# A softmax pass in a graph network: GpSimd weights half of the features, and a dense pipeline starts its newest group first

## The reference

```python
x_j = h[dst] + ee                       # h = x @ W_lin + b_lin, ee = edge_attr @ W_edge + b_edge, two heads of 64
alpha = (x_i * att_i).sum(-1) + (x_j * att_j).sum(-1)
alpha = jnp.where(alpha >= 0, alpha, NEG_SLOPE * alpha)
e = jnp.exp(alpha - segment_max(alpha, src, N)[src])
alpha = e / (segment_sum(e, src, N)[src] + 1e-16)
out = segment_sum(x_j * alpha[:, :, None], src, N).mean(axis=1) + bias
x = _layernorm(x + out)
```

## Time and profile before

| what | before |
|---|---|
| median of 3 runs | 10380.73 us |
| lowest and highest | 10374.76 and 10389.13 us |
| profiled execution, first to last instruction (its span) | 11537.7 us |
| DVE busy | 6821.8 us, 59% |
| POOL busy | 6567.8 us, 57% |
| ACT busy | 4714.2 us, 41% |
| PE busy | 3146.5 us, 27% |

### The profile page before, as it was taken

One profiled execution on the slowest core, in us unless ns is written; L12 is line 12 of the kernel. 1 busy time (PEld: TensorE's weight loads), 2 busy tenths in 40 slices (PEclk: granted clock), 3 DMA queues, 4 the chain that ended last, 5 costly groups with the idle time before them and its releaser, 6 DMA issues. The chain is left out here.

```text
span 11537.7 us, 92744 instructions
## 1 busy us (share of the span) xinstructions
PE 3146.5 (27%) x19432; PEld 2586.9 (22%) x19432; DVE 6821.8 (59%) x9436; ACT 4714.2 (41%) x6523; POOL 6567.8 (57%) x6626
## 2 busy tenths in 40 slices
PE   1111588882000000000023555555554200000002
PEld 1111477772000000000013444444443100000001
DVE  6777666664222311159962777777775566666664
ACT  1111466661211111137731666666662343334342
POOL 5656666665677777730023666666662466666663
PEclk9999767675555555555555677776775655555555
DMA  3332322222333323235522444444441666666662
GB/s 91 88 83 78 80 60 71 71 82 26 121 112 111 107 94 106 103 125 207 205 104 52 117 118 124 117 116 122 118 117 39 194 202 201 199 202 205 203 201 70
DMA packets 722783, 1395.92 MB, mean 121 GB/s; under 512 B 409552, under 2 KB 439453, under 8 KB 715095
## 3 DMA queue, kind: packets, MB, share of 16 engines
q0 software_dynamic: 287072, 587.19, 19.4%
q1 hardware_dynamic: 406786, 639.32, 17.0%
q10 hardware_dynamic: 28852, 168.65, 4.0%
HBM read 827.48 MB, written 602.51 MB: 124 GB/s over the span
## 5 line engine op out<-in xcount | busy, mean ns | idle before, releaser
L822 POOL DMA_INDIRECT l_rows<-in_x,l_idx x1568 | 1613.7, 1029 | 1010.1 <-issue 431.0
L2445 POOL DMA_INDIRECT l_rows<-table,l_idx x1568 | 1487.5, 949 | 1032.2 <-issue 483.2
L1925 POOL DMA_INDIRECT l_rows<-h,l_idx x1568 | 1540.3, 982 | 882.1 <-issue 442.4
L1303 POOL DMA_INDIRECT rows<-l_rows,l_idx x1568 | 1548.9, 988 | 554.0 <-issue 526.3
L1960 PE MATMUL l_made<-l_kv_w,l_rows_t 128*128 128x256 f32 x3136 | 1117.3, 514 | 1041.1 <-ACT l_kv L1990 402.5
L1960 PEld LDWEIGHTS l_made<-l_kv_w,l_rows_t 128*128 128x128 f32 x3136 | 761.2, 259 | 1279.5 <-issue 1147.1
L2521 ACT ACTIVATE l_lifted<-l_rows,l_up 128x256 f32<-128x256 f32 x1568 | 653.2, 463 | 824.0 <-DVE l_half_low L2473 527.1
L1698 PE MATMUL l_wide<-l_diag,l_ones 128*128 128x384 f32 x4 | 3.3, 926 | 3218.0 <-DVEq L1728 3218.0
L1259 ACT COPY l_rows<-l_run 128x1792 f32<-128x1792 f32 x56 | 191.6, 3421 | 1636.1 <-POOLq L88 1359.5
L1292 DVE TENSOR_TENSOR l_rows<-l_run,l_weights_ps 128x56 f32<-128x56 f32 x56 | 12.0, 215 | 1371.0 <-POOLq L88 1168.7
L1698 PEld LDWEIGHTS l_wide<-l_diag,l_ones 128*128 128x128 f32 x4 | 1.0, 312 | 3218.9 <-DVEq L1728 3218.9
(11 more groups left out here) (393 smaller groups left out, 12672.9 us busy)
## 6 DMA issues: line engine op xcount, KB each, us to landing
sums<-l1s_out ACTq DMA_DIRECT2D x56, 1988.0 KB, 7.1
sums<-l_out SPq DMA_DIRECT2D x112, 924.0 KB
spread<-zeros SPq DMA_DIRECT2D x28, 3612.0 KB
l_spread<-spread SPq DMA_DIRECT2D x112, 903.0 KB
l1s_rows<-rows SPq DMA_DIRECT2D x56, 1008.0 KB, 4.7
spread<-zeros SPq DMA_DIRECT2D x56, 938.0 KB
l_spread<-spread SPq DMA_DIRECT2D x56, 938.0 KB
sums<-l_out ACTq DMA_DIRECT2D x56, 896.0 KB
```

The lines of the kernel that those rows point to most:

```text
L822: pool.indirect_dma_start(rows[:, b, t], None, a["x"], bass.IndirectOffsetOnAxis(ap=idx[:, b, t:t + 1], axis=0)) \
L1303: pool.indirect_dma_start(g["rows1_d"], bass.IndirectOffsetOnAxis(ap=idx[:, b, t:t + 1], axis=0), rows[:, b, t], None).then_inc(sent[b], 16)
L1925: pool.indirect_dma_start(rows[:, c.r, t, 0:C], None, g["h2_d"], bass.IndirectOffsetOnAxis(ap=idx[:, c.r, t:t + 1], axis=0)).then_inc(got[ ...
L2445: pool.indirect_dma_start(rows[:, b, t], None, g["table3_d"], bass.IndirectOffsetOnAxis(ap=idx[:, b, t:t + 1], axis=0)) \
```

## The change

**In the softmax pass** each part's two products are made by two engines and its scan is cut in two.

- DVE weights the features for head 0 only (`weighed_low`, PSUM), and raises the new semaphore `begun` behind the copy of the last column. GpSimd weights those for head 1 (`weigh`), into `weighed_high`, which is the second head's half of the old `scale` tensor in SBUF. It may write part n when `begun` says that DVE has left the scans of the part before last, and when the exponentials are there.
- `scale_low` stays in SBUF; the scales of head 1 go to `scale_high`, a single buffer in PSUM.
- DVE scans head 0 (2030 elements), waits for GpSimd (`high_weighed`) and for ACT (`high_ready`), and scans head 1 (2030 elements).
- ACT makes the scales in two functions. `low` is as before for one head. `high` waits for the end of the last part's second scan, since the buffer is single, copies that part's last column (a new instruction, 70 elements), and then writes `scale_high`. The order of ACT's turn becomes high(c,1), exponentials, store(c,0), low, high(c+1,0), store(c,1), low(c+1,1).
- `rows_used` now counts two engines. DVE clears `scale_high` once at the start.

```diff
-                        for head in range(H):
-                            last = v.tensor_tensor(data[:, head, :, 1:].rearrange("p f t -> p t f"), rows[:, b, at, 0:F],
-                                                   exp[:, b, 1, head, at].unsqueeze(2).to_broadcast([P, T, F]), ALU.mult)
-                        last.then_inc(rows_used[b][n], 1)
-                        v.tensor_copy(data[:, :, :, 0:1], run[:, 1 - n, :, :, T:T + 1])
-                        wait(v, scale_ready[n], c.at + 1)
+                        v.tensor_tensor(weighed_low[:, :, 1:].rearrange("p f t -> p t f"), rows[:, b, at, 0:F],
+                                        exp[:, b, 1, 0, at].unsqueeze(2).to_broadcast([P, T, F]), ALU.mult).then_inc(rows_used[b][n], 1)
+                        v.tensor_copy(weighed_low[:, :, 0], run[:, 1 - n, 0, :, T]).then_inc(begun, 1)
+                        wait(v, low_ready[n], c.at + 1)
                         wait(v, copied[n], c.at + 1)
                         v.drain()
...
+                        wait(v, high_weighed, c.at * PARTS + (n + 1))
+                        wait(v, high_ready[n], c.at + 1)
+                        v.tensor_tensor_scan(run[:, n, 1].rearrange("p f t -> p (f t)"), scale_high.rearrange("p f t -> p (f t)"),
+                                             weighed_high[:, n].rearrange("p f t -> p (f t)"), 0.0, ALU.mult, ALU.add).then_inc(scanned[n], 1)
                         v.drain()
...
+                def weigh(c, n):
+                    at = slice(n * T, (n + 1) * T)
+                    wait(pool, exp_ready[c.b], c.h + 2)
+                    if not (isinstance(c.g, int) and c.at == 0 and n == 0):
+                        wait(pool, begun, c.at * PARTS + n)
+                    pool.tensor_tensor(weighed_high[:, n, :, 1:].rearrange("p f t -> p t f"), rows[:, c.b, at, 0:F],
+                                       exp[:, c.b, 1, 1, at].unsqueeze(2).to_broadcast([P, T, F]), ALU.mult).then_inc(rows_used[c.b][n], 1)
+                    pool.drain().then_inc(high_weighed, 1)
...
+                def high(c, n):
+                    wait(act, scanned[1 - n], c.at + (n + 1))
+                    nc.scalar.copy(weighed_high[:, n, :, 0], run[:, 1 - n, 1, :, T])
+                    nc.scalar.copy(scale_high[:, :, 1:], exp[:, c.b, 0, 1, n * T:(n + 1) * T].unsqueeze(1).to_broadcast([P, F, T])).then_inc(high_ready[n], 1)
...
                 def turn(c, after):
+                    high(c, 1)
+                    if after:
+                        exponentials(after)
                     store(c, 0)
                     if after:
-                        exponentials(after)
-                        scales(after, 0)
+                        low(after, 0)
+                        high(after, 0)
                     store(c, 1)
                     if after:
-                        scales(after, 1)
+                        low(after, 1)
```

**In the dense pipelines** the loop over the stages runs the other way, on PE and on ACT, so that at step s the newest group is turned first and the product of the group before follows:

```diff
         for step in range(len(self.groups) + self.stages - 1):
-            for k in reversed(range(self.stages)):
+            for k in range(self.stages):
```

**Between ordering and layer 0** stands a second `clear_semaphores`:

```diff
+        ordering(nc, a, sem, dict(locals()))
+        clear_semaphores()
         norm = Normalise(sem, "l01")
-        ordering(nc, a, sem, dict(locals()))
```

More of the change, by code:

```diff
@@ L1425, in source_order_sums @@
         exp = s.sb("l1s_exp", [P, 2, 2, H, S])
-        data = s.ps("l1s_data", [P, H, F, T + 1])
+        weighed_low, scale_high = (s.ps(f"l1s_{n}", [P, 4 * 512])[:, 0:F * (T + 1)].rearrange("p (f t) -> p f t", t=T + 1)
+                                   for n in ("weighed_low", "scale_high"))
+        scale_low, weighed_high = scale[:, :, 0], scale[:, :, 1]
         outb = s.sb("l1s_out", [P, PARTS, T, W + H])
@@ L1500, in _ @@
                 v.tensor_copy(tail[:, W:W + H], top[:, UNROLL - 1, :, S])
+            @block.gpsimd
+            def _(pool):
+                def weigh(c, n):
[6 more added lines that the diff above has]
+                    pool.drain().then_inc(high_weighed, 1)
+                pool.wait_ge(set_up, 1)
+                for r in range(UNROLL):
+                    for n in range(PARTS):
+                        weigh(Chunk(0, r), n)
+                with pool.Fori(1, NB // UNROLL) as q:
+                    for r in range(UNROLL):
+                        for n in range(PARTS):
+                            weigh(Chunk(q, r), n)
             @block.scalar
@@ L1511, in exponentials, with low @@
                     wait(act, exp_ready[c.b], c.h + 2)
-                def scales(c, n):
+                def low(c, n):
                     wait(act, scanned[n], c.at + 1)
-                    for head in range(H):
-                        last = nc.scalar.copy(scale[:, n, head, :, 1:], exp[:, c.b, 0, head, n * T:(n + 1) * T].unsqueeze(1).to_broadcast([P, F, T]))
-                    last.then_inc(scale_ready[n], 1)
+                    nc.scalar.copy(scale_low[:, n, :, 1:], exp[:, c.b, 0, 0, n * T:(n + 1) * T].unsqueeze(1).to_broadcast([P, F, T])).then_inc(low_ready[n], 1)
+                def high(c, n):
+                    wait(act, scanned[1 - n], c.at + (n + 1))
+                    nc.scalar.copy(weighed_high[:, n, :, 0], run[:, 1 - n, 1, :, T])
+                    nc.scalar.copy(scale_high[:, :, 1:], exp[:, c.b, 0, 1, n * T:(n + 1) * T].unsqueeze(1).to_broadcast([P, F, T])).then_inc(high_ready[n], 1)
                 def store(c, n):
@@ L1811, in scalar @@
         for step in range(len(self.groups) + last - 1):
-            for k in reversed(range(last)):
+            for k in range(last):
                 i = step - k
```

18 lines of the change are left out of this document (10 added, 8 removed).

## The result

The changed kernel takes 10198.83 us (median of 4 runs, 10194.06 to 10207.38) against 10383.55 for the kernel before in the same session: ratio 0.9821 [0.9807, 0.9835]. The forecast was 10232, its range 10180 to 10295. The time lies in the range and 33 us under the point, at the rival "TensorE's clock rises" (10194).

A forecast was written before the change was run, and what follows sets the result against it. VectorE was taken to bound the softmax pass, and waits between stages the output products. Terms -115 + 4 - 21 - 10 - 2.5 - 6 + 2 = -149 took 10380.7 to 10232 us, range 10180 to 10295.

The forecast's parts named there:

- TensorE's clock rises: Rival, faster: in both output products, gapless TensorE work raises the clock, -38 us over some 34 steps, 10194 us; chance 0.12.
- The pass: Softmax pass: VectorE's part falls from 13.4 to 11.35 us, a chunk to 26.0, -115 us over 56 parts.
- too slow: Rival, softmax pass: GpSimd's product exceeds 8.9 us and VectorE stands for the rest; at 13 us 10461; chance 0.05.
- half of it: Rival, softmax pass: GpSimd's product about 9.9 us or ScalarE at 27 us a chunk, +56, 10288 us; chance 0.11.
- taking turns: Rival, softmax pass: GpSimd and VectorE do not work together, only the pipelines gain, 10350 us; chance 0.03.
- The start of the pass: Softmax pass start: clearing 2030 elements 1.7 us, GpSimd's and VectorE's first products together +2; together +4 (1.7 to 9).
- the prediction's own sign of error: Softmax pass: the forecast is wrong if VectorE's product or scores lengthen beside GpSimd's product; no size given.
- The dense pipelines: Output products: the wait goes, step 2.63 instead of 3.50 us at clock 0.50; -21 in layer 1, -10 in layer 2.
- The MLP: MLP: nearly full already, with 0.21 us of wait a step; -2.5 us (0 to -3.9).
- The query product: Query product: GpSimd, issuing 49 transfers at 987 ns and more each, sets the pace; 0 us.
- The root product: Root product: waits 0.94 us a step but also stands 18.2 us at once; -6 us, between 0 and -11.
- The second clear: A second clear leaves VectorE idle for at most 2.23 us more; +2 us (0 to 2.2).

The follow-up runs named there:

- e1: Changed kernel with the old order of TensorE's and ScalarE's work in the pipelines, leaving the pass and the second clear: 10279.94 us against 10393.57, ratio 0.9895.
- e5: Changed kernel, VectorE signalling GpSimd at the start of its own product instead of after the copy behind it: 11603.07 us on a slower chip, ratio to before 0.9833.
- e6: Changed kernel with the first head's weighted features in SBUF instead of PSUM: 11659.38 us, ratio to the kernel before 0.9881.
- e2: Kernel before with only the new order in the pipelines: 10317.49 us against 10393.57, ratio 0.9931.
- e4: Kernel before, old order, two unread 128x128 products after each step's turns in layer 1's output product: that stage took 79.0 us.
- e10: Kernel before, old order, four unread 128x128 products after each step's turns in layer 1's output product: that stage took 57 us.
- e7: Changed kernel, TensorE's turns in layer 2's attention pass held until ScalarE's first scale copy of the chunk two before: 11577.15 us on a slow chip, ratio 0.9804.
- e11: Changed kernel, held-back attention turns, unread TensorE products up to the start of both output products: 11438.85 us against 11654.21 on a slower chip, ratio 0.9801.
- e0: The kernel before, unchanged, timed and profiled a second time: 10382.33 us.
- e8: The changed kernel, unedited, timed again over five rounds beside the kernel before: 10200.02 us against 10386.37, ratio 0.9826.
- e3: Changed kernel, ScalarE's store copy going through the running sums in the order of the output instead of the input: 10205.60 us, ratio 0.9826.
- e9: Changed kernel with held-back turns in the attention pass and 26 and 40 unread TensorE products ahead of the output products: 10156.01 us, ratio to before 0.9784.

## Why the prediction was right, and where it failed

**The pass: right, a little too small.** Forecast -115 us and +4 at its start, measured -119.5 from first to last scan (e1, with all but the pipelines: -114 in all). The part is 11.24 us and not 11.35: two waits behind the first scan cost nothing, since the second scan starts 0.08 us before the first one's end. GpSimd's product took 3.81 us where 4.4 was assumed between 2.2 and 8.6, and lay under the scan as the order said. So "too slow", "half of it" and "taking turns" did not happen. ScalarE waits 73.1 us for the scan, 12.3 of them once at the start; the other 60.8 / 26 = 2.3 us a chunk are what the sum had left (26.0 - 23.7).

**The start of the pass** had the collision, in another place than forecast: not the first products, but `scores` of the next chunk, where in the changed kernel a copy took 3.76 us instead of 0.23 and in e1 the instruction ahead of it 3.77:

```profile
4661.26 3.81 POOL L1516 TENSOR_TENSOR l1s_scale<-l1s_rows,l1s_exp 128x1960 f32<-128x1960 f32 x1 [24.66 <-ACT l1s_exp L1537]
4661.38 3.76 DVE L1466 COPY l1s_hold_data<-l1s_side 128x112 f32<-128x112 f32 x1
```

```profile
4674.84 3.74 POOL L1516 TENSOR_TENSOR l1s_scale<-l1s_rows,l1s_exp 128x1960 f32<-128x1960 f32 x1 [25.52 <-ACT l1s_exp L1537]
4674.88 3.77 DVE L1465 TENSOR_SCALAR l1s_hold_keep<-l1s_side 128x112 f32<-128x112 f32 x1 [1.93 <-DMA l1s_side<-spreada]
```

The Trainium skill's "SBUF — State Buffer", section "Who interferes with whom", has the two engines shut each other out for a whole instruction, copies among them, and lets the order of issue decide which one waits. These rows, e5 and e6 agree: GpSimd's product was held where VectorE's product or scan had started 0.01 to 0.05 us before it, and VectorE's small instruction where GpSimd's product had started 0.04 to 0.12 us before it. This second kind happened once in a run, for 3.5 us; it is also the prediction's own sign of error, that scores lengthen beside GpSimd's product, in a form too rare to matter.

**The dense pipelines: the step that failed.** The prediction priced the closed gap at the low clock alone. It kept TensorE at 0.50 and gave its rise a chance of 0.12, because TensorE had worked 20.99 of 21 us at 0.50 in another stage. In the new order the clock rises in both output products: -46.4 and -24.0 instead of -21 and -10. Of the 46.4 about 25 are the waits and the overlap of the kinds of product (25 steps of 3.44 at 2.45 us), the other 21 the clock; the runs on the order alone (e2, -76) and on the gap alone (e4, e10) bear it out. The row that spoke against it still stands: the stretch behind the root product has no gap and stays at 0.50 for 21 us in the changed kernel too, and the root product ahead of it, which keeps a wait of 0.16 us a step, stays at 0.50 for all of its 38 us. So a stretch without a gap may rise 4.5, 17 or 66 us in (7 to 22 us in layer 1's output product over the eight profiles with the new order), or not within 21, and one that didn't is weak evidence against. The rule of the Trainium skill's "TensorE: Matmul & The Clock Gate", Part 1, that sustained activity releases the throttle, deserved more than it got: both output products agree with it (granted clock 0.77 and 0.82), this one stretch does not.

**Smaller terms.** The step at the low clock was 2.45 us, not 2.63: the eight products take 1.60 us start to start when their weights are ready, not 1.77. The MLP gave 5.9 (forecast 2.5). The query product fell from 38 to 20 us where 0 was forecast, but the 48 transfers that GpSimd issues from its rows take 61.6 us in either kernel, as the prediction had it, and 7.0 is left of the whole stretch. The root product gave 8.7 (forecast 6), and the end of the kernel gave 8.3 of it back: GpSimd's last transfers end 66.1 us behind the start of the root product in both kernels (10243.1 to 10309.2 and 10056.9 to 10123.0), so the forecast's -6 should have been 0. Stalls like the 18.18 us of the earlier trace rows, three of 6 to 29 us in the root product, stand in every profile of over 11300 us (before, e4 to e7, e11) and in none of the others. The second clear (+2) can't be told: VectorE is idle for 14.8 to 15.9 us ahead of layer 0 without it (before, e0, e2) and for 15.8 to 17.0 with it (e1, after, e8).

**What the forecast did not have** is the attention pass, 2053 to 2095 us by its cadence, and with it, as it seems, steps of some 42 us between the times of one kernel. The profiles of the changed kernel (after, e8) and of e1 and e3 are all at 2094 to 2097; why the pass should favour that is open. It took some 19 us off the gain against e0.

**Where luck helped.** The rival "TensorE's clock rises" is the account that held, and its two output products (-69) are close to the -70 measured. That its whole time, 10194, is met within 5 us is luck: the pass and what leads to it gave 14 us more than it had, the query product 7 and the MLP 3, the root product 6 less, and the attention pass took 19 back. One sum of the prediction is off without consequence: its own parts put the lower end of the forecast's range at 10214 and not at 10205.

## What to carry to other kernels

Price a closed gap on TensorE twice, at the present clock and at the high one, and give the second a real chance: here the waits were worth 25 us and the clock 21 more. Moving elementwise work to GpSimd was free here where its time lay under scans that read one operand from PSUM. A collision cost nothing where VectorE's instruction had started first and GpSimd had slack; where GpSimd's had started first, VectorE stood for the rest of it (3.5 us), so arrange who starts first. Where the same kernel's times fall into two groups, look for a loop with two steady cadences before reading small differences; holding back an engine that ran too early was worth 44 us here, as much as the new order in layer 1's output product.

## What the runs showed of the hardware

- GpSimd's product of 128x1960 took 3.81 us, and VectorE's 2.21. With VectorE's instruction 0.05 us ahead, GpSimd's took 5.80 beside that product and 7.83 beside a scan with both inputs in SBUF (e5, e6). With GpSimd's ahead, a VectorE instruction on 128x112 took 3.76 us instead of 0.23 (after, e1).
- VectorE's strided product of 128x1960 took 2.21 us into PSUM and 3.70 into SBUF, with GpSimd idle on either side (after, e6).
- TensorE's clock was back at 1.2 GHz after a pause of 5.16 us and still at 2.4 after 0.85 us (e9, e11).
- The same program took 10386 us on one chip and 11654 and 11802 on two others. The softmax pass, bound by VectorE, was equal within 0.1 us (715.3 and 715.4 from first to last scan in e8, e7 and e11); where many rows move, in layer 3, transfers ran at 202 GB/s instead of 236 (e7, e8). Each chip was used in one session only, so chip and session are not told apart.
